# A post-norm layer with attention and 64 experts: wo and z fetched in attention's last pair, shared units moved ahead, the last norm inside the experts' block

## The chip, the cores and the metric

The kernel runs on one core of a Trainium2 chip. The time is the device time of one execution in microseconds (us), as the median over runs on the same inputs; lower is better. Before the change it is 2542.3 us, the median of three runs (2539.97 to 2544.57).

A core has five engines that matter here: PE (TensorE, the matmuls), DVE (VectorE), ACT (ScalarE), POOL (GpSimd) and SP (SyncE, which here only issues DMAs and waits). Each runs its own instructions in order and meets the others at semaphores.

## The reference

One layer on x of 2048 tokens by 512. Attention has 16 heads of 128; the norm stands behind each of the two sums, and has no weights.

```python
scores = jnp.einsum('biph,biqh->biqp', k, q)
masked = scores * mask - jnp.float32(10000000000.0) * (1.0 - mask)
attn = jax.nn.softmax(masked / jnp.sqrt(jnp.float32(d_head)), axis=-1)
z = jnp.einsum('biqp,biph->biqh', attn, v)
out = jnp.einsum('df,bqf->bqd', W_O, z_flat)
...
x = _layernorm(x + attention(x, W_K, W_Q, W_V, W_O))
x = _layernorm(x + ffn(x, gate_w, w1, w2, w3, sw1, sw2, sw3))
```

In `ffn` a softmax over 64 experts picks 6 for each token. An expert takes its first 128 tokens, computes `silu(x w1) * (x w3)` (352 wide) and from it `w2`, and the result is added to the token's row with its gate. A shared expert, 704 wide, is added for every token.

## The kernel before

All large products are made at the precision of fp32 from three matmuls: each operand is split into a rounded part "hi" and the rest "lo", and the passes are hi*hi, lo*hi and hi*lo. The hi part is a copy on ACT; the lo part is a subtraction on DVE, which needs it. So an operand that comes from memory goes DMA, ACT, DVE, PE.

The program has three blocks, one behind the other, with a barrier of all engines between them.

**Attention.** The heads go as 8 pairs, and in each pair the queries as 4 chunks of 512. A table of steps written by hand (`attention_plan`) sets the order on every engine: projections ("job"), scores and their exponentials, "turns" (transposes of the probabilities, which ACT copies as `pT_hi`, L428, and DVE completes as `pT_lo`, L512) and the products with v (L653). The last pair has no projections of a next pair beside it, so its last stretch is turns and products alone. z goes to `z_dram`, tile by tile.

**Projection, routing, experts** (`route_and_experts`). POOL first makes constants (up to L994) for which PE waits. SP fetches the first tile of z (L1081) and `w_o` in 8 groups of two heads; ACT splits z (L1200) and then the groups (L1192), DVE behind it (L1614, L1609). Then PE takes 16 tiles of 128 tokens: the output projection (L1385, 48 matmuls a tile), the norm, the routing and the scattering of rows. Tile 1 of z is fetched once `z_lo` of tile 0 is made. Behind the tiles stand 8 "lead" units of the shared expert, for 4 of the 16 tiles.

Then comes a loop of 4 bodies with 22 units each: 16 experts ("e") and 6 shared units ("s", a half of the shared expert for one tile), in the order `PATTERN = "eeseeseeees" * 2`. A unit on PE is its up products (L1473), the down products of the unit before (L1513), and the transposes of the next unit's rows (L1449) and of its activations (L1454). The experts' weights stream through 8 raw slots: SP fetches a piece (L1133), ACT and DVE split it. Which step fetches and splits which piece stands in a table (`pieces_of_step`); those of the next body's first expert, and at the very start of the loop seven `EARLY` ones, come ahead. POOL adds each expert's result to `sums_dram` by an indirect DMA (L1059) and each shared tile's by a plain one (L1066), one behind the other.

**The last norm** (`combine`). SP loads the 16 tiles of `sums_dram` (L1910). For groups of four tiles DVE measures (L1930, L1934), takes ACT's square root (L1918) through six small steps to 1/sqrt (L1942 to L1958), and normalises (L1963). ACT issues the stores (L1921).

## Time and profile before

| | us |
|---|---|
| median of three runs | 2542.3 |
| profiled execution | 2545.8 |
| its span | 2543.9 |
| PE busy in it | 2438.9 (96%) |
| DVE busy | 1738.1 (68%) |
| ACT busy | 1425.4 (56%) |
| last matmul of the attention block ends | 1620.4 |
| first matmul of the projection | 1635.43 |
| last matmul of all ends | 2498.6 |
| SP starts to load for the last norm | 2509.97 |

The profile is one execution. Its times count from the span's start. In a row of the timeline stand the start, the duration, the engine, the line, what is written and read, and in brackets the idle time before it and what ended it. A busy engine can be waited for or not; a time in which PE is idle is the first thing to look for, because PE is busy for 96% of the span.

### The profile page before, as it was taken

How to read it: one execution, taken by the hardware profiler on the slowest of the kernel's cores; microseconds unless marked ns; L12 is line 12 of the kernel's file. 1: busy time of each engine (PE TensorE's matmuls, PEld its weight loads, DVE VectorE, ACT ScalarE, POOL GpSimd, SP SyncE). 2: the span in 40 equal slices, each digit the busy share in tenths (PEclk: the TensorE clock that was granted, in tenths of full speed). 3: DMA queues.
4: the chain of work that ended last, by engine and by line, in shares of the span. 5: the costliest groups of instructions: out<-in, count | busy, mean ns of one | idle time of the engine just before them, and what ended most of it. 6: DMA issues, size and time to landing. Idle time of an engine off the chain costs nothing. (4 is left out here: it accounts for less than half of the span.)

```text
span 2543.9 us, 40857 instructions
## 1 busy us (share of the span) xinstructions
PE 2438.9 (96%) x14202; PEld 2117.1 (83%) x14202; DVE 1738.1 (68%) x3656; ACT 1425.4 (56%) x3199; POOL 346.6 (14%) x366
## 2 busy tenths in 40 slices
PE   6999999999999999999999999799999999999992
PEld 5888888888888888888888888588889988898982
DVE  4666666566567567657567566578758887888884
ACT  3555455455456456446456455455447776777771
POOL 0000000000000000000000000167621211222121
PEclk9999999999999999999999999899999999999996
DMA  7421411421330331322322220488659999999995
GB/s 263 134 63 57 140 59 56 131 69 28 124 106 26 127 95 37 124 67 65 120 74 65 82 90 26 151 287 315 221 152 310 307 298 291 307 309 305 312 295 153
DMA packets 193421, 397.00 MB, mean 156 GB/s; under 512 B 23674, under 2 KB 73210, under 8 KB 182977
## 3 DMA queue, kind: packets, MB, share of 16 engines
q1 hardware_dynamic: 163456, 330.69, 38.6%
q0 software_dynamic: 27456, 59.51, 10.0%
q10 hardware_dynamic: 2304, 4.20, 0.4%
q8 instruction: 114, 1.87, 0.3%
q14 instruction: 91, 0.74, 0.1%
HBM read 296.45 MB, written 106.48 MB: 158 GB/s over the span
## 5 line engine op out<-in xcount | busy, mean ns | idle before, releaser
L428 ACT ACTIVATE pT_hi<-turned 128x512 fp32r<-128x512 f32 (+3 forms) x640 | 334.2, 535 | 270.9 <-PE turned L638 268.5
L417 ACT ACTIVATE probs<-bank,neg_max 128x512 f32<-128x512 f32 (+3 forms) x640 | 396.6, 626 | 109.5 <-DVE neg_max L506 104.5
L512 DVE TENSOR_TENSOR pT_lo<-turned,pT_hi 128x512 fp32r<-128x512 f32 (+3 forms) x640 | 377.5, 603 | 75.1 <-ACT pT_hi L428 71.7
L498 DVE TENSOR_REDUCE max_part<-bank 128x1 f32<-128x512 f32 (+2 forms) x576 | 345.2, 620 | 96.0 <-PE bank L621 84.0
L608 PE MATMUL bank<-x_sb,w_hi 128*128 128x512 f32 x1024 | 323.4, 397 | 20.1 <-ACT ident_bf L393 13.4
L638 PE MATMUL turned<-ident,probs 128*128 128x128 f32 x2176 | 329.2, 273 | 0.1
L638 PEld LDWEIGHTS turned<-ident,probs 128*128 128x128 f32 x2176 | 264.4, 141 | 49.2 <-PE bank L597 0.3
L653 PE MATMUL z_ps<-pT_hi,v_hi 128*128 128x512 f32 (+3 forms) x640 | 255.0, 398 | 2.5 <-DVE pT_lo L512 1.9
L621 PE MATMUL bank<-k_lo,q_hi 128*128 128x512 f32 (+2 forms) x640 | 254.3, 397 | 0.0
L621 PE MATMUL bank<-k_hi,q_hi 128*128 128x512 f32 (+2 forms) x640 | 253.3, 396 | 0.0
L1764 DVE TENSOR_TENSOR up_lo<-w_raw,up_hi 128x704 fp32r<-128x704 f32 x256 | 217.3, 887 | 39.2 <-ACT up_hi L1256 38.1
L608 PEld LDWEIGHTS bank<-x_sb,w_hi 128*128 128x128 f32 x1024 | 189.8, 190 | 57.5 <-issue 13.4
L653 PE MATMUL z_ps<-pT_hi,v_lo 128*128 128x512 f32 (+3 forms) x640 | 233.8, 365 | 0.0
L621 PE MATMUL bank<-k_hi,q_lo 128*128 128x512 f32 (+2 forms) x640 | 233.7, 365 | 0.0
L653 PE MATMUL z_ps<-pT_lo,v_hi 128*128 128x512 f32 (+3 forms) x640 | 233.2, 364 | 0.0
L283 POOL DMA_DIRECT2D inv_dram<-inv x64 | 35.0, 546 | 1353.1 <-DVE inv L524 1353.1
L608 PE MATMUL bank<-x_sb,w_lo 128*128 128x512 f32 x512 | 200.9, 392 | 0.0
L597 PE MATMUL bank<-w_hi,x_sb 128*128 128x256 f32 x1024 | 193.8, 285 | 1.7 <-ACT probs L417 1.7
L1256 ACT ACTIVATE up_hi<-w_raw 128x704 fp32r<-128x704 f32 x250 | 184.8, 785 | 3.2 <-DMA w_raw<-in_w 3.1
L597 PEld LDWEIGHTS bank<-w_hi,x_sb 128*128 128x128 f32 x1024 | 164.1, 193 | 3.9 <-DVE probs L471 2.1
L1059 POOL DMA_INDIRECT sums_dram<-y_sb,token x64 | 110.7, 1730 | 390.4 <-DMA sums_dram<-y_sb,token 252.7
L597 PE MATMUL bank<-w_lo,x_sb 128*128 128x256 f32 x512 | 145.6, 284 | 0.0
(202 smaller groups left out, 5150.4 us busy)
## 6 DMA issues: line engine op xcount, KB each, us to landing
w_raw<-in_w SPq DMA_DIRECT2D x256, 352.0 KB, 5.7
x_sb<-x_parts SPq DMA_DIRECT2D x62, 1024.0 KB, 6.1
w_raw<-in_w SPq DMA_DIRECT2D x128, 256.0 KB, 5.6
rows_in<-gathered_x SPq DMA_DIRECT2D x64, 263.5 KB, 5.7
spread_sb<-inv_dram POOLq DMA_DIRECT2D x64, 256.0 KB, 3.5
z_dram<-z_sb SPq DMA_DIRECT2D x64, 256.0 KB, 2.3
z_raw<-z_dram SPq DMA_DIRECT2D x16, 1024.0 KB, 5.1
w_raw<-in_w_qkv SPq DMA_DIRECT2D x32, 384.0 KB, 8.6
```

The costliest lines, as they stand in the source:

```text
L417: nc.scalar.activation(probs[:, u % 2, r, kc * CHUNK:kc * CHUNK + used], bank[:, job_at["s", h, c, r, kc] % BANKS, 0:used], ACT.Exp, bias= ...
L428: nc.scalar.activation(pT_sb[0][:, n % TURNS, lo_col:], turned[:, n % TURNS, lo_col:], ACT.Copy).then_inc(turn_hi, 1)
L498: nc.vector.reduce_max(max_part[:, row % ROWS, kc:kc + 1], bank[:, job % BANKS, 0:used], axis=AX_X).then_inc(part_done, 1)
L512: nc.vector.tensor_tensor(pT_sb[1][:, n % TURNS, lo_col:], turned[:, n % TURNS, lo_col:], pT_sb[0][:, n % TURNS, lo_col:].bitcast(F32), AL ...
L597: mark = nc.tensor.matmul(dst[:, t * 2 * DH:(t + 1) * 2 * DH], x_sb[:, a, dt, rows_], w_sb[b][:, dt, 4 * DH:], start=(dt == 0 and (a, b) = ...
L608: mark = nc.tensor.matmul(dst, w_sb[a][:, dt, first:first + DH], x_sb[:, b, dt, :], start=(dt == 0 and (a, b) == PASSES[0]), stop=(dt == D ...
L621: mark = nc.tensor.matmul(dst[:, 0:width], q_sb[a][:, h, r * P:(r + 1) * P], k_sb[b][:, h, kc * CHUNK:kc * CHUNK + width], start=(a, b) == ...
L638: mark = nc.tensor.transpose(turned[:, n % TURNS, r * P:(r + 1) * P], probs[:, u % 2, r, j * P:(j + 1) * P], ident[:])
L653: mark = nc.tensor.matmul(z_ps[:, first * P:], v_sb[a][:, j, h * DH:(h + 1) * DH], pT_sb[b][:, n % TURNS, first * P:], start=(j == 0 and ( ...
L1059: nc.gpsimd.indirect_dma_start(sums_dram, bass.IndirectOffsetOnAxis(ap=token4[:, n:n + 1], axis=0), y_sb[:, n % 2], None, bounds_check=las ...
L1256: nc.scalar.activation(dst_of(0, n % 2, p, up_w, down_w), raw_of(raw, q % SLOTS_RAW, p), ACT.Copy).then_inc(w_hi, 1)
L1764: nc.vector.tensor_tensor(dst_of(1, n % 2, p, up_w, down_w), raw_of(raw, q % SLOTS_RAW, p), dst_of(0, n % 2, p, up_w, down_w).bitcast(F32) ...
```

## The change

It has three parts.

**1. Room and an early start.** The SBUF tensors of the stages are laid out in one function, `rooms`, so that `wo_raw`, `z_raw` and the split z and wo lie over attention's x, w, k and probabilities. In attention's last pair SP fetches all of `w_o` behind the last job, waits for the stores of z and fetches z's first tile. ACT splits that tile in 4 parts and the first two of the 8 groups of wo between its turns; DVE makes their rests between its own. The other six groups are split in the second block. The wait for `gate_w` goes from PE's start to the first logits.

On ACT, at the end of attention; before (`probs` are the exponentials, `pT_hi` the turns):

```order
L428 ACTIVATE pT_hi<-turned 128x384
L417 ACTIVATE probs,sums<-bank,neg_max 128x512 x2
L428 ACTIVATE pT_hi<-turned 128x256
L428 ACTIVATE pT_hi<-turned 128x128
L428 ACTIVATE pT_hi<-turned 128x512 x13
L428 ACTIVATE pT_hi<-turned 128x384
```

And after:

```order
L514 ACTIVATE pT_hi<-turned 128x384
L523 ACTIVATE z_hi<-z_raw 128x512
L503 ACTIVATE probs,sums<-bank,neg_max 128x512 x2
L514 ACTIVATE pT_hi<-turned 128x256
L523 ACTIVATE z_hi<-z_raw 128x512
L514 ACTIVATE pT_hi<-turned 128x128
L523 ACTIVATE z_hi<-z_raw 128x512
L514 ACTIVATE pT_hi<-turned 128x512
L523 ACTIVATE z_hi<-z_raw 128x512
L514 ACTIVATE pT_hi<-turned 128x512 x5
L531 ACTIVATE wo_hi<-wo_raw 128x1024
L514 ACTIVATE pT_hi<-turned 128x512 x2
```

Six splits (the second wo group follows) now stand among the turns; in the second block ACT begins with wo's group 2.

**2. Units.** `PATTERN` is turned by one place, so each body begins with a shared unit; the table of pieces is turned with it, and 2 pieces in place of 7 are early. The tile of each body's first shared unit is fetched by SP two units before the body before ends, behind a wait for the up products of that body's fifth shared unit. POOL's adds of shared tiles come at other places (`tile_after`), so that three experts' adds are last instead of a shared one.

On PE, where the loop begins; before (the first two rows end the last lead unit, `rows_in` are the rows of the first expert's tokens):

```order
L1454 MATMUL t_even<-ident,h_sb 128x128 x2
L1454 MATMUL t_even<-ident,h_sb 96x128
L1449 MATMUL t_odd<-ident,rows_in 128x128 x4
L1473 MATMUL h_even<-up_hi,eT_hi 128x352
L1473 MATMUL h_even<-up_lo,eT_hi 128x352
```

And after, with the end of the unit, 17 rows further on:

```order
L1596 MATMUL t_even<-ident,h_sb 128x128 x2
L1596 MATMUL t_even<-ident,h_sb 96x128
L1615 MATMUL h_even<-s_up_hi,sT 128x352
L1615 MATMUL h_even<-s_up_lo,sT 128x352
...
L1615 MATMUL h_even<-s_up_hi,sT 128x352
L1591 MATMUL t_odd<-ident,rows_in 128x128 x4
L1655 MATMUL ys_ps<-s_down_hi,hT_hi 128x512
```

The transposes of the first expert's rows stood directly ahead of its up products; now a whole up part of a shared unit goes ahead of them.

**3. The last norm** is in the second block, without a barrier ahead of it. SP itself waits for POOL's adds, loads, and issues the stores. The groups are 4, 4, 4, 2 and 2 tiles. ACT normalises tiles 0 to 13 as `inverse * x + shift`, DVE the last two; one of the six steps is folded into another and one makes the shift.

On DVE, for one group; before:

```order
L1942 TENSOR_SCALAR varc<-mvc 128x4
L1945 RECIPROCAL guessc<-rootc 128x4
L1948 TENSOR_TENSOR newton_partc<-guessc 128x4
L1930 BN_STATS statsc<-sums_in 128x6
L1951 SCALAR_TENSOR_TENSOR newton_partc<-newton_partc,varc 128x4
L1955 TENSOR_SCALAR newton_partc<-newton_partc 128x4
L1958 TENSOR_TENSOR inversec<-newton_partc,guessc 128x4
L1934 BN_AGGR mvc<-statsc 128x2
L1963 TENSOR_SCALAR yc<-sums_in,mvc,inversec 128x512
```

And after:

```order
L2011 BN_STATS statsc<-sums_in 128x6
L2026 RECIPROCAL guessc<-rootc 128x4
L2015 BN_AGGR mvc<-statsc 128x2
L2029 TENSOR_TENSOR newton_partc<-guessc 128x4
L2011 BN_STATS statsc<-sums_in 128x6
L2032 SCALAR_TENSOR_TENSOR newton_partc<-newton_partc,varc 128x4
L2015 BN_AGGR mvc<-statsc 128x2
L2036 SCALAR_TENSOR_TENSOR inversec<-newton_partc,guessc 128x4
L2011 BN_STATS statsc<-sums_in 128x6
L2040 SCALAR_TENSOR_TENSOR shiftc<-mvc,inversec 128x4
```

The steps now stand singly between measurements, and no normalising row stands between the groups: it has gone to ACT.

The diff, cut to its core:

```diff
+def rooms(nc, ctx):
+    with ExitStack() as part:
+        x_sb = sb("x_sb", [P, 2, DT, CHUNK], F32R, part)
+        w_raw = sb("w_raw", [P, 3, 6 * DH], F32, part)
+        w_sb = [sb(f"w_{n}", [P, DT, 6 * DH], F32R, part) for n in ("hi", "lo")]
+        k_sb = [sb(f"k_{n}", [P, 2, SEQ], F32R, part) for n in ("hi", "lo")]
+        probs = sb("probs", [P, 2, RPC, SEQ], F32, part)
+    with ExitStack() as part:
+        wo_raw = sb("wo_raw", [P, HEADS, DM], F32, part)
...
@@ attention: tables of the added splits
+        z_hi_part = {(0, 3, 13): 0, (0, 3, 14): 1, (0, 3, 15): 2, (1, 3, 0): 3}
+        z_lo_part = {(1, 3, 1): 0, (1, 3, 2): 1, (1, 3, 3): 2, (1, 3, 4): 3}
+        wo_hi_group = {(1, 3, 5): 0, (1, 3, 7): 1}
+        wo_lo_group = {(1, 3, 6): 0, (1, 3, 9): 1}
@@ attention, SP, behind the last job
+                            for g in range(HEADS // GROUP):
+                                sp.dma_start(room.wo_raw[:, g * GROUP:(g + 1) * GROUP], w_o[:, g * GROUP:(g + 1) * GROUP]
+                                             ).then_inc(begun.wo_in[g], 16)
+                            for n in range(2):
+                                sp.wait_ge(z_out[n], 8 * n_units * PAIRS + 16)
+                            sp.dma_start(room.z_raw[:], z_dram[0]).then_inc(begun.z_in, 16)
@@ route_and_experts
-    PATTERN = "eeseeseeees" * 2
+    PATTERN = "seeseeeseee" * 2
-    LEAD_SPLITS = {4: EARLY[0:2], 5: EARLY[2:4], 6: EARLY[4:5]}
-    LATE_SPLITS = EARLY[5:]
+    LEAD_SPLITS = {4: EARLY}
@@ POOL
-            tile_after = {5 - 1: 0, 10 - 1: 1, NE - 1: 2}
+            tile_after = {1: 0, 7: 1, 12: 2}
@@ SP
-            load_z(0, 0)
-            for g in range(HEADS // GROUP):
-                sp.dma_start(wo_raw[:, g * GROUP:(g + 1) * GROUP], w_o[:, g * GROUP:(g + 1) * GROUP]
-                             ).then_inc(wo_in[g], 16)
             sp.wait_ge(z_lo, 1)
             load_z(0, 1)
...
-            tile_step = {unit_of["s", 0]: (0, -1), unit_of["s", 2] - 2: (1, -1), unit_of["s", 4] - 2: (2, unit_of["s", 1])}
+            sp.wait_ge(up_ready, lead_unit(5) + 1)
+            load_tile(FIRST, tile_slot(0))
+            tile_step = {unit_of["s", 2] - 2: (1, -1), unit_of["s", 4] - 2: (2, unit_of["s", 1]),
+                         NU - 2: (NST, unit_of["s", 5])}
...
+            for n in range(2):
+                sp.wait_ge(y_stored[n], (16 * NE // 2) * BODIES)
+                sp.wait_ge(ys_stored[n], slot_count(BODIES - 1, 2 - n, 16))
+            for t in range(TILES):
+                sp.dma_start(sums[:, t], sums_dram[t * P:(t + 1) * P]).then_inc(loaded[t], 16)
@@ ACT
-            split_z(0, 0)
-            for g in range(HEADS // GROUP):
+            for g in range(FIRST_GROUPS, HEADS // GROUP):
                 split_wo(g)
...
+            for g, tiles_ in enumerate(ENDS):
+                act.wait_ge(mean_ready, tiles_[-1] + 1)
+                part = slice(tiles_[0], tiles_[-1] + 1)
+                nc.scalar.activation(roots[:, part], end_mv[:, part, 1], ACT.Sqrt, bias=end_eps[:]).then_inc(roots_ready, 1)
+                if g:
+                    act.wait_ge(newton_step, END_STEPS * g)
+                    for t in ENDS[g - 1]:
+                        end_normalise(t)
```

## Rows read from the trace of the kernel before

**Rows 1.** The page, part 1: busy time, share of the span, instructions.

```profile
PE 2438.9 (96%) x14202; PEld 2117.1 (83%) x14202; DVE 1738.1 (68%) x3656; ACT 1425.4 (56%) x3199; POOL 346.6 (14%) x366
```

**Rows 2.** Windows: length, busy PE, PEld, DVE, ACT, POOL, granted clock, DMA share, GB/s.

```profile
1600.00:1610.00 10.00, 9.41 (x50) 7.87 (x50) 5.87 (x12) 4.19 (x8) 0.11 (x1) 0.83 0.10 28
1610.00:1620.00 10.00, 10.00 (x62) 8.49 (x62) 5.92 (x10) 4.63 (x9) 0.97 (x2) 1.00 0.11 26
1635.43:1647.94 12.51, 12.51 (x48) 9.95 (x48) 8.86 (x10) 8.56 (x8) 0.00 (x0) 0.88 0.75 298
```

**Rows 3.** Timeline across the blocks' border: start, duration, engine, line, idle before.

```profile
1620.12 0.27 PE L653 MATMUL z_ps<-pT_hi,v_lo 128*128 128x128 f32 x1
1625.05 0.32 SPq L1081 DMA_DIRECT2D z_raw<-z_dram  x1
1626.58 0.14 POOL L994 IOTA mine_i<- 128x16 int32 x1
1629.84 1.91 ACT L1200 ACTIVATE z_hi<-z_raw 128x2048 fp32r<-128x2048 f32 x1 [10.37 <-DMA z_raw<-z_dram]
1631.86 2.29 DVE L1614 TENSOR_TENSOR z_lo<-z_raw,z_hi 128x2048 fp32r<-128x2048 f32 x1 [6.30 <-ACT z_hi L1200]
1632.55 1.06 ACT L1192 ACTIVATE wo_hi<-wo_raw 128x1024 fp32r<-128x1024 f32 x1 [0.80 <-DMA wo_raw<-in_w_o]
1633.83 1.06 ACT L1192 ACTIVATE wo_hi<-wo_raw 128x1024 fp32r<-128x1024 f32 x1 [0.22 <-DMA wo_raw<-in_w_o]
1635.43 0.77 PE L1385 MATMUL o_ps<-wo_hi,z_hi 128*128 128x512 f32 x1 [15.03 <-DVE wo_lo L1609]
```

**Rows 4.** Timeline, PE, from tile 0 to tile 1 of the projection.

```profile
1647.55 0.39 PE L1385 MATMUL o_ps<-wo_hi,z_lo 128*128 128x512 f32 x1
1649.78 0.50 PE L1385 MATMUL o_ps<-wo_hi,z_hi 128*128 128x512 f32 x1 [1.84 <-DVE z_lo L1614]
```

**Rows 5.** Waits over the whole program: who, for what, sum, count, mean.

```profile
PE h_even L1473 <- issue: 6.0, 4, 1.5
ACT up_hi L1256 <- DMA w_raw<-in_w: 3.1, 5, 1.5
```

**Rows 6.** Timeline near the first body's end: fifth shared unit's up, SP's step.

```profile
2009.58 0.40 PE L1473 MATMUL h_odd<-s_up_hi,sT 128*128 128x352 f32 x1
2015.87 0.33 SPq L1144 DMA_DIRECT2D rows_in<-gathered_x  x1
```

**Rows 7.** Timeline, the experts' end.

```profile
2496.84 1.55 POOL L1059 DMA_INDIRECT sums_dram<-y_sb,token  x1 [4.27 <-ACT y_sb L1321]
2498.16 0.40 PE L1513 MATMUL ys_ps<-s_down_hi,hT_lo 96*128 96x512 f32 x1
2502.25 0.92 POOL L1066 DMA_DIRECT2D sums_dram<-ys_sb  x1 [3.85 <-DMA sums_dram<-y_sb,token]
2509.97 8.10 SPq L1910 DMA_DIRECT2D sums_in<-sums_dram  x16
```

**Rows 8.** Timeline, the last norm, and one of the experts' results on ACT.

```profile
2495.39 0.68 ACT L1321 ACTIVATE y_sb<-y_ps,gate 128x512 f32<-128x512 f32 x1
2512.50 0.69 DVE L1930 BATCH_NORM_STATS2 statsc<-sums_in 128x6 f32<-128x512 f32 x1 [2.39 <-DMA sums_in<-sums_dram]
2513.33 0.67 DVE L1930 BATCH_NORM_STATS2 statsc<-sums_in 128x6 f32<-128x512 f32 x1
2516.64 1.28 ACT L1918 ACT_TABLE_LOAD   x1 [20.57 <-DVE mvc L1934]
2517.94 0.30 ACT L1918 ACTIVATE rootc<-mvc,epsc 128x4 f32<-128x4 f32 x1
2537.02 0.16 DVE L1942 TENSOR_SCALAR varc<-mvc 128x4 f32<-128x4 f32 x1
2538.06 0.16 DVE L1948 TENSOR_TENSOR newton_partc<-guessc 128x4 f32<-128x4 f32 x1
2538.86 1.92 DVE L1963 TENSOR_SCALAR yc<-sums_in,mvc,inversec 128x512 f32<-128x512 f32 x4
```

More of the change, by code:

```diff
@@ L1 @@
+from collections import namedtuple
 from contextlib import ExitStack
@@ L76, with first_sems, sem @@
+def first_sems(nc, ctx):
+    def sem(name):
+        return ctx.enter_context(nc.semaphore(name))
+    return FirstSems(sem("z_in"), sem("z_hi"), sem("z_lo"), [sem(f"wo_in{n}") for n in range(HEADS // GROUP)],
+                     sem("wo_hi"), sem("wo_split"))
 ORDER = (
@@ L438, in body @@
                         turn(i, *step[2:])
+                        if last and step[2:] in z_hi_part:
+                            first_z_hi(i, z_hi_part[step[2:]])
+                        if last and step[2:] in wo_hi_group:
+                            first_wo_hi(i, wo_hi_group[step[2:]])
                     if step[0] == "wsplit" and not last:
@@ L542, in body @@
                         low(i, *step[2:])
+                        if last and step[2:] in z_lo_part:
+                            first_z_lo(z_lo_part[step[2:]])
+                        if last and step[2:] in wo_lo_group:
+                            first_wo_lo(wo_lo_group[step[2:]])
                     if step[0] == "inverse":
@@ L742, in route_and_experts @@
     assert EARLY == list(range(EARLY[0], NQ))
-    LEAD_SPLITS = {4: EARLY[0:2], 5: EARLY[2:4], 6: EARLY[4:5]}
-    LATE_SPLITS = EARLY[5:]
-    assert all(pieces[q][0] % 2 for q in LATE_SPLITS) and not any(pieces[q][0] % 2 for q in EARLY[:5])
+    LEAD_SPLITS = {4: EARLY}
+    assert not any(pieces[q][0] % 2 for q in EARLY)
     SLOTS_RAW = 8
@@ L875, in route_and_experts @@
         t_at = {job: n for n, job in enumerate(tjobs)}
+        z_in, z_hi, z_lo, wo_in, wo_hi, wo_split = begun
         waited = sem("waited3")
@@ L936, in route_and_experts @@
         ys_stored = [sem(f"ys_stored{n}") for n in range(2)]
+        eps_ready = sem("eps_ready")
+        loaded = [sem(f"loaded{t}") for t in range(TILES)]
+        stats_ready = sem("stats_ready")
+        mean_ready = sem("mean_ready")
+        roots_ready = sem("roots_ready")
+        newton_step = sem("newton_step")
+        y_ready = sem("y_ready")
+        y_ready_dve = sem("y_ready_dve")
+        stored = sem("stored")
         block = ctx.enter_context(nc.Block())
@@ L1327, in body @@
                         turned(i, ("x", 0))
-                    if first and u == 0:
-                        for q in LATE_SPLITS:
-                            split_first(q)
                     if not (first and u < 2):
@@ L1336, in body @@
                     silu(i, u)
+                    if first and u == 0:
+                        for m in range(2):
+                            act.wait_ge(rows_left[m], rows_of(TILES - 2 + m))
+                        for m in range(NB):
+                            act.wait_ge(x1_stored[m], 16 * TILES // NB)
+                        for m in range(2):
+                            act.wait_ge(t_stored[m], 32 * TILES // 2)
                     if u + 1 < NU and UNITS[u + 1][0] == "e":
@@ L1943, in invert @@
                 if n == 1:
-                    dve.wait_ge(rooted, g + 1)
-                    ins = nc.vector.reciprocal(guess[:, part], root[:, part])
+                    dve.wait_ge(roots_ready, g + 1)
+                    ins = nc.vector.reciprocal(guess[:, part], roots[:, part])
                 if n == 2:
@@ L1978, in _ @@
-                    if g < GROUPS:
-                        mean(t)
-                    if g:
-                        normalise(t - GROUP)
+                    end_measure(t)
+                    steps = (FOUR if len(tiles_) == 4 else TWO)[n] if g else ()
+                    for m in steps[:1]:
+                        invert(g - 1, m)
+                    end_mean(t)
+                    for m in steps[1:]:
+                        invert(g - 1, m)
+            for n in range(END_STEPS):
+                invert(len(ENDS) - 1, n)
```

339 lines of the change are left out of this document (167 added, 172 removed).

## The prediction

> **What bounds the kernel now.** I read page part 1 first: PE is busy for 96% of the span, ACT and DVE for much less [rows 1]. So the change can only gain where PE stands idle and after its last matmul. Those places come from PE's idle times in the timeline: 15.03 us between attention and projection, 1.84 us ahead of tile 1 [rows 3, 4], 6.0 us in four waits at the body starts [rows 5], and the end, from the last matmul at 2498.56 to 2543.9 [rows 7, 8]. That is 68 us of idle time. The three parts of the change are aimed at these places and leave PE's matmuls as they are, in number and shape.
>
> A difference within 0.2%, about 5 us, cannot be told from no change. The sum is made against the profiled execution, 2545.8 us. The median of the runs is 2542.3, so 3.5 is taken off at the end.
>
> **A. Attention's tail.** ACT gets 4 splits of 128x512 and 2 of 128x1024, DVE as many. From the rows, a 128x1024 split on ACT is 1.06 and z's 128x2048 is 1.91, on DVE 2.29 [rows 3]; a quarter of these is about 0.5 and 0.6. ACT gets some 4 x 0.5 + 2 x 1.06 = 4.1 us, DVE 4 x 0.6 + 2 x 1.2 = 4.8. In 1600 to 1620 ACT is busy for 4.2 and 4.6 of each 10 us, DVE for 5.9 and 5.9 [rows 2], so there is room. But turns come in a chain PE, ACT, DVE, PE, and a split in front of one makes it late. In 1600 to 1610 PE is already idle for 0.6 us; later it is never idle [rows 2], and has turns made ahead. Laying the tail end to end with these durations I get +1.5. The bounds are 0 and +4 (all of ACT's part shows, as the chain is through ACT).
>
> **B. The gap between the blocks.** The last matmul of attention ends at 1620.12 + 0.27 = 1620.4. The first of the projection is at 1635.43, after DMA of z (issued 1625.05), z_hi at 1629.84, z_lo at 1631.86, and the wo splits behind them [rows 3]. After the change z's tile 0 and four heads of wo are split by then. What is left stands in front of all of them: z's last store and the barrier, which let SP begin at 1625.05, and POOL's constants, made from there to 1626.58 + 0.14 = 1626.72 [rows 3], for which PE still waits. So the first o_ps is at about 1626.8, 8.6 earlier. Does wo keep up? ACT makes a group in 1.27 (1632.55 to 1633.83 [rows 3]). Six groups from 1625.1 are done at 1632.7, DVE's last one about 1.2 later, 1633.9. PE comes to the eighth group after 14 of 16 heads of a tile that takes 12.51 [rows 2], at 1626.8 + 10.9 = 1637.7. No wait. The bounds are -9 (POOL's constants a little earlier) and -7 (a late group or barrier costs 1.5). The granted clock of tile 0 was 0.88 [rows 2], below 1 because PE starts at 1.2 GHz after the idle time; I leave that as it is, since 6.4 us of idle time remain.
>
> **C. The wait ahead of tile 1.** 1.84 us for z_lo [rows 4], which comes because tile 1 is fetched only after tile 0's z_lo, and z_lo is behind ACT's eight groups. Now the fetch goes out at 1625.5. Landed 4.8 later (1625.05 to 1629.84 [rows 3]) it waits for ACT's six groups, 1632.7; z_hi 1.91 and z_lo 2.29, started 2.02 behind z_hi [rows 3], make 1637.0. Tile 0 ends at 1626.8 + 12.5 = 1639.3. The wait goes: -1.8, with -1 as the other bound.
>
> **D. Body starts.** PE waited four times 1.5 us "on issue" for the first h_even [rows 5]: the transposes of the expert's rows were directly in front of its up products, so that ACT and DVE had to copy them with PE standing. Now a shared unit's up part stands between, 3.8 us long (24 matmuls at 0.16, as h_even and h_odd go in the loop). All of it goes: -6.0, with -5 as the bound. What takes its place? The first tile of the next body is fetched at SP's step NU-2, behind a wait for the fifth shared unit's up. On the rows of before that up began at 2009.58 and lasts 3.8 us, done by 2013.5, and SP comes to the step at 2015.87 [rows 6]. SP is therefore not held, by 2.3 us, and the row loads and weights queued behind are not late. Seven early pieces become two, so five are fetched and split a unit later. The pieces then have a whole shared unit to land in.
>
> **E. The experts' end.** The last matmul ends at T = 2498.56. POOL issues the last expert's add at 2496.84, T - 1.7, and the shared add goes out when that has landed, 2502.25, T + 3.7: one indirect add takes 5.4. Then come the shared add, the barrier and the block's start, and SP loads at 2509.97, T + 11.4 [rows 7]. After, the last three units are experts. The second to last add lands at T + 3.7 as before; the last takes another 5.4, T + 9.1; SP itself waits for it and loads at T + 9.2. So -2.2: an indirect add takes the place of the plain one, and eats most of what the barrier gives. The bounds are -3.2 (add of 4.4) and -0.6 (add of 7).
>
> **F. The last norm.** Before, from L = 2509.97 to 2543.9 is 33.9, and the last normalising ends at 2538.86 + 1.92 = 2540.78, 3.1 before the end [rows 8]. DVE is the engine in the chain. After, per tile it measures in 0.83 (2512.50 to 2513.33) and per group makes six steps of 0.20 (four from 2538.06 to 2538.86) [rows 8]. Group 0 is measured by L + 6.7, where ACT's root was asked for at 2516.64 [rows 8]. Then groups of 4, 4, 2 and 2 cost 4 x 0.83 + 1.2 = 4.5, 4.5, 2 x 0.83 + 1.2 = 2.9 and 2.9: L + 11.1, 15.6, 18.5, 21.4. The last group's steps with its root take 1.84 (2537.02 to 2538.86), DVE's two last tiles 2 x 0.48, and 3.1 is added as before [rows 8]: L + 27.3. So -6.7. ACT's part is 14 tiles at about 0.57 (y_sb, the same shape, is busy for 0.68 [rows 8], and back to back a little less), 2.3 a group against DVE's 4.5. The loads take 8.1 to issue [rows 7], and the last measurement is at L + 20, so they aren't late. Bounds -8 (store's tail shorter) and -5 (DVE and ACT each slower by a quarter in places).
>
> **Sum.** +1.5 - 8.6 - 1.8 - 6.0 - 2.2 - 6.7 = -23.8. Of the profiled 2545.8 this leaves 2522.0; of the median 2518.5. All bounds together are 0 - 9 - 1.8 - 6 - 3.2 - 8 = -28 and 4 - 7 - 1 - 5 - 0.6 - 5 = -14.6, so 2514 to 2528.
>
> **Rivals.**
> R1, the end gives less. The last indirect add is as slow as 7 us (E -0.6), and F gives -3 only, because the small steps, strung singly between measurements, each wait for the one before. For it: each step takes what the one before has written, and one that starts too early stands. Against it: a measurement of 0.69 or its second part stands between them, longer than the 0.20 from one step to the next [rows 8]. 1.5 - 8.6 - 1.8 - 6.0 - 0.6 - 3 = -18.5, or 2524.
>
> R2, the weights come late. Five pieces less are ahead at the loop's start. For it: ACT did wait for w_raw in the loop, so the stream has no large reserve. Against it: only five times, for 3.1 us in all [rows 5]. If each of the five missing pieces costs one such wait of 1.5, and the five existing ones double, 7.5 + 3.1 = 10.6 come on top: 2529.
>
> R3, ACT holds the last norm. The first root waits for a table load of 1.28, the root following 1.30 behind its start [rows 8]. If the load held ACT for twice as long, DVE, which asks for the first reciprocal at about L + 8.5, would stand for 1.4 us; and if the normalising went at y_sb's full 0.68 a tile [rows 8] and not at 0.57, four tiles would end 0.4 later. That is -22.0, or 2520.3. The Trainium skill, "ScalarE: Activation LUTs", section "What ACT_TABLE_LOAD costs", speaks for it: it counts a drain of 1.38 us with each load, 2.66 in all, and some 93 ns for each operand that is one value per partition, of which the new normalise has two. By that rule the sum is -22.0. The trace of before shows the load and no drain behind it, 1.30 to the root, so my sum goes without.
>
> R4, the side above. The splits in attention's tail stand in the chain one behind another, 4.1 + 4.8 = 8.9 us, and their holes drop PE to 1.2 GHz for the 23 us that the tail has left, which doubles them: 8.9 + 23 = +32 in place of +1.5. 2518.5 + 30.4 = 2549, slower. It decides from +25.3, where A eats all other terms. For it: 1600 to 1610 is granted 0.83 with 0.6 us idle [rows 2]. Against it: in the next 10 us the clock is 1.00 and PE is never idle, with ACT busy for less than half.
>
> R5, the room isn't free when it should be: the fetches into attention's old room wait until the last jobs are done, and would hold up SP. The last pair's stores come before the z fetch on SP's queue, and nothing that PE needs stands behind them. Should z's parts be late by more than the turns allow, B falls to -5, and the sum to -20.2: 2522.
>
> **How the numbers follow.** The forecast's own case (2514 to 2523) has 0.62, R1 0.14, R3 0.08, R5 0.05, R2 0.07 and R4 0.04. 2518.5 is the time of the likeliest. The range of 2511 to 2528 takes in R1, R3 and R5 and the bounds, and a little below, since an estimate of six terms can be short on both sides; R2 and R4 are left out with 0.11 and the rest of the tails. Faster by over 0.2% (below 2537.2) is all but R4 and half of a further mishap: 0.94. Within 0.2%: 0.03, slower: 0.03.
>
> **What would show it.** First o_ps 6.4 us behind the last z_ps, not 15; no wait for z_lo at tile 1; no "issue" wait at h_even; attention's last z_ps at 1621 to 1622 and not past 1625, at a granted clock near 1; the first sums_in issue at T + 9.2 with the last indirect add landing just before; 27.3 us from there to the end, with DVE free of idle times over 0.7. It would be wrong if the tail's holes grow, if ACT's w_raw waits in the loop go past 10 us, or if y_ready of tile 13 comes behind DVE's last two tiles.

## The result, and the profile after

| | before | changed |
|---|---|---|
| median of the runs, first comparison (5 and 5 runs) | 2542.3 us | 2525.9 us (2518.3 to 2530.3) |
| ratio, 95% interval | | 0.993 (0.9906 to 0.9954) |
| median, second comparison (17 and 6 runs) | 2546.2 | 2523.0 (2520.5 to 2527.6) |
| ratio, 95% interval | | 0.9913 (0.9888 to 0.9938) |
| span of the profiled execution | 2543.9 | 2528.5 |

The change is faster by 16 us in one comparison and 23 in the other, where 23.8 were forecast. The two ratios agree within their intervals. The runs of the changed kernel lie 7 to 12 us apart in a comparison; what this spread goes with is shown below.

Two corrections to what stands ahead. The last number of the waits in [rows 5] is the longest one and not the mean. And `PATTERN` is not only turned by one place. The strings in the diff show it: before, a period has experts in runs of 2, 2 and 4 between shared units, after it 2, 3 and 3. And the third shared tile's add now stands ahead of the body's last three experts.

**The span by terms.** T is the end of the last matmul, L is SP's first load for the last norm.

| stretch | before | after | difference | forecast |
|---|---|---|---|---|
| start to the last z_ps (A) | 1620.39 | 1620.35 | 0.0 | +1.5 |
| to the first o_ps (B) | 15.04 | 6.39 | -8.7 | -8.6 |
| to T (C and D) | 863.1 | 864.5 | +1.3 | -7.8 |
| T to L (E) | 11.4 | 11.8 | +0.4 | -2.2 |
| L to the end (F) | 33.9 | 25.5 | -8.5 | -6.7 |

So the start and the norm gave what they should, or more, and the middle gave nothing. PE is now busy for 97%, with the same number of matmuls as in [rows 1]:

```profile
PE 2440.2 (97%) x14202; PEld 2119.3 (84%) x14202; DVE 1731.5 (68%) x3651; ACT 1436.3 (57%) x3217; POOL 350.9 (14%) x366
```

The border of the blocks, timeline of the changed kernel (answers [rows 3]):

```profile
1620.08 0.27 PE L778 MATMUL z_ps<-pT_hi,v_lo 128*128 128x128 f32 x1
1626.54 0.14 POOL L1114 IOTA mine_i<- 128x16 int32 x1
1626.74 0.80 PE L1525 MATMUL o_ps<-wo_hi,z_hi 128*128 128x512 f32 x1 [6.38 <-POOL mine_i L1114]
```

The tail that ends there, as a window (its columns as in [rows 2]), is at full clock:

```profile
1610.00:1620.00 10.00, 9.97 (x62) 8.20 (x60) 7.47 (x12) 5.48 (x10) 0.55 (x2) 1.00 0.10 26
```

PE waits for POOL's last constant and nothing else, and tile 1 starts without a wait: in the changed kernel's timeline no idle time over 0.25 us stands between this row and the lead units. That is [rows 4] gone.

The waits of the whole program (answer to [rows 5]): for whom, sum, count, longest.

```profile
POOL sums_dram L1179 <- DMA sums_dram<-y_sb,token: 284.5, 45, 8.4
PE t_even L1596 <- DVE h_sb L1929: 10.0, 3, 5.0
ACT up_hi L1388 <- DMA w_raw<-in_w: 3.8, 6, 1.3
```

The row "h_even <- issue" of [rows 5] is gone: the body starts no longer wait, as forecast. The weights, which rival R2 suspected, are as they were (3.1 before, 3.8 now). But PE's wait for h_sb has grown from 4.0 us in two waits to 10.0 in three, and the first row, POOL waiting for its own DMA 45 times, is the largest wait of any engine in the loop. Both rows stood in the trace of before as well; I had not read them:

```profile
POOL sums_dram L1059 <- DMA sums_dram<-y_sb,token: 252.7, 42, 8.3
PE t_even L1454 <- DVE h_sb L1792: 4.0, 2, 3.0
```

From the first o_ps to T, PE's idle time went from 20.3 us to 19.2 only, and its busy time from 842.8 to 845.3. That is the +1.3 of the table, where 7.8 us of idle time were to go.

**What the 10.0 us are.** The longest but one of them, at 2049, in the timeline of the changed kernel, POOL, ACT and PE:

```profile
2030.17 0.91 POOL L1186 DMA_DIRECT2D sums_dram<-ys_sb  x1 [6.66 <-DMA sums_dram<-y_sb,token]
2032.57 0.68 ACT L1445 ACTIVATE y_sb<-y_ps,gate 128x512 f32<-128x512 f32 x1
2038.41 2.00 POOL L1179 DMA_INDIRECT sums_dram<-y_sb,token  x1 [7.32 <-issue]
2044.89 0.69 ACT L1445 ACTIVATE y_sb<-y_ps,gate 128x512 f32<-128x512 f32 x1 [5.51 <-issue]
2049.16 0.87 PE L1596 MATMUL t_even<-ident,h_sb 128*128 128x128 f32 x3 [4.00 <-DVE h_sb L1929]
```

Read it from the top. POOL's adds go to the same tensor, so in the kernel each waits until the one before has landed: a shared tile's at 2030.17 lands after 7.4 us, and an expert's follows at 2038.41, 8.2 us behind it. There are two result buffers (`y_sb`). ACT comes to the next result at 2039.4 (2044.89 less the idle 5.51), but its buffer is held by the add issued at 2038.41, and that lands 6.4 us later, at 2044.8. ACT stands until then; behind it in its queue is the act_sb of the next unit, behind this DVE's h_sb, and PE waits 4.0 us for that. Then PE starts at 1.2 GHz, seen in the granted clock of 0.50:

```profile
2048.00:2053.00 5.00, 3.84 (x14) 3.79 (x15) 4.97 (x13) 3.58 (x8) 1.56 (x1) 0.50 0.99 273
```

So such a wait costs more than its idle time: the matmuls behind it come every 0.29 us in place of 0.16 for 4 us, which by these numbers is some 1.9 us more (an estimate).

**The end**, timeline of the changed kernel (answers [rows 7]):

```profile
2486.92 1.61 POOL L1179 DMA_INDIRECT sums_dram<-y_sb,token  x1 [4.33 <-issue]
2490.81 0.39 PE L1655 MATMUL y_ps<-down_hi,hT_lo 96*128 96x512 f32 x1
2492.58 1.55 POOL L1179 DMA_INDIRECT sums_dram<-y_sb,token  x1 [4.05 <-ACT y_sb L1445]
2498.24 1.56 POOL L1179 DMA_INDIRECT sums_dram<-y_sb,token  x1 [4.10 <-DMA sums_dram<-y_sb,token]
2503.03 8.25 SPq L1312 DMA_DIRECT2D sums_in<-sums_dram  x16
```

The adds of the last three experts are issued 5.66 us apart. Each lands 4.7 to 4.9 us after its issue, and the next goes out 0.8 us behind that. The last but one starts at T + 1.4 and not at T - 1.7, because the third last is under way until 2491.8. The bracket of its row names ACT's y_sb, but the result that ended at 2492.5 on ACT is the last expert's; this add's own was ready at 2488.7:

```profile
2488.04 0.68 ACT L1445 ACTIVATE y_sb<-y_ps,gate 128x512 f32<-128x512 f32 x1
2491.85 0.69 ACT L1445 ACTIVATE y_sb<-y_ps,gate 128x512 f32<-128x512 f32 x1 [3.13 <-PE y_ps L1655]
```

SP loads at once when the last has landed, without a barrier. What the barrier gave was eaten by one link of this chain.

**The last norm**, DVE and ACT at its end (answers [rows 8]):

(the row of four and the row of 0.80 are the same group, the latter its last)

```profile
2509.71 1.28 ACT L1507 ACT_TABLE_LOAD   x1 [17.17 <-DVE mvc L2015]
2511.01 0.30 ACT L1507 ACTIVATE rootc<-mvc,epsc 128x4 f32<-128x4 f32 x1
2520.19 2.92 ACT L1499 ACTIVATE yc<-sums_in,shiftc,inversec 128x512 f32<-128x512 f32 x4
2522.31 0.80 ACT L1499 ACTIVATE yc<-sums_in,shiftc,inversec 128x512 f32<-128x512 f32 x1
2523.01 0.28 ACT L1507 ACTIVATE rootc<-mvc,epsc 128x2 f32<-128x2 f32 x1
2523.33 0.17 DVE L2026 RECIPROCAL guessc<-rootc 128x2 f32<-128x2 f32 x1 [1.52 <-ACT rootc L1507]
2524.31 1.00 DVE L2062 TENSOR_SCALAR yc<-sums_in,mvc,inversec 128x512 f32<-128x512 f32 x2
```

DVE is through all measurements, and the steps of the group before the last, at L + 18.8 where I had L + 21.4: 2.6 us sooner, since the small steps between measurements cost about 0.1 and not 0.2 us each. At the very end ACT is late, as R3 had it: the root stands behind four normalisings, and DVE waits 1.52, which makes the last group's steps 0.7 longer than forecast.

### The profile page after: what moved, and what is told of

It is laid out like the page before. It is cut to its first block and busy times, and to the rows that moved or that the text cites. A ratio compares the mean times of both kernels' runs of the same rounds, so it can differ in the third digit from the quotient of the medians.

```text
span 2528.5 us, 40864 instructions
## 1 busy us (share of the span) xinstructions
PE 2440.2 (97%) x14202; PEld 2119.3 (84%) x14202; DVE 1731.5 (68%) x3651; ACT 1436.3 (57%) x3217; POOL 350.9 (14%) x366
## 5 line engine op out<-in xcount | busy, mean ns | idle before, releaser
L1179 POOL DMA_INDIRECT sums_dram<-y_sb,token x64 | 116.2, 1816 | 398.8 <-DMA sums_dram<-y_sb,token 284.5
```

Source lines behind the costliest of these rows:

```text
L1179: nc.gpsimd.indirect_dma_start(sums_dram, bass.IndirectOffsetOnAxis(ap=token4[:, n:n + 1], axis=0), y_sb[:, n % 2], None, bounds_check=las ...
```

## The experiments

Theory A, formed from the rows above: **POOL's adds to the sums are a chain that bounds the loop beside PE.** A body has 16 experts' adds and 3 shared ones. From the first to the last of the loop's 76 adds the changed kernel takes 591.4 us, 7.89 a link, so 19 links are 149.8 us. PE's body without the waits is 146.6 (experiment 9; 148.4 in experiment 1, with the 1.5 of the old body start). Taking PE's wait away leaves it waiting for the chain. The mean of a link alone doesn't prove this, as it is the loop's time divided by the adds, whichever of the two bounds it. The brackets say more: in the changed kernel 57 of the 76 issues follow a landing, in that of before 53, and some that name ACT or "issue" do so too, like those at 2038.41 and 2492.58 above. The experiments that shorten the chain decide. Theory B: the new order is a gain, and the microseconds were lost to the weights or the DMA engines. In the third theory a single place of the order is at fault (experiment 2).

The main numbers of the profiled executions, all described below. A link is the mean distance between POOL's 76 issues in the loop; where PE waits for nothing it is the loop's pace and not what the chain needs. The last column is the median of the runs; that of before lay between 2542 and 2548 in the several comparisons.

| kernel | T | link | L | span | median |
|---|---|---|---|---|---|
| before | 2498.6 | 7.83 | 2509.97 | 2543.9 | 2546 |
| changed | 2491.2 | 7.89 | 2503.03 | 2528.5 | 2525.9 |
| changed, again | 2479.5 | 7.72 | 2493.38 | 2518.7 | 2523.0 |
| order back | 2481.2 | 7.75 | 2488.96 | 2515.0 | 2521.8 |
| third tile's add later | 2494.8 | 7.92 | 2504.98 | 2530.5 | 2536.1 |
| shared adds out | 2474.7 | 7.64 (9.09 between its 64 adds) | 2483.69 | 2509.3 | 2512.3 |
| four buffers | 2476.8 | 7.64 | 2486.85 | 2512.6 | 2524.8 |
| order alone | 2497.5 | 7.85 | 2515.82 | 2549.8 | 2550.5 |
| plain writes | 2477.2 | 7.59 | 2481.88 | 2507.4 | 2509.1 |

From L to the end the kernels of this table with the new norm take 25.3 to 26.0 us, so L decides, and L is when the chain ends.

**1. The order of before, back in the changed kernel.**

```diff
-    PATTERN = "seeseeeseee" * 2
+    PATTERN = "eeseeseeees" * 2
...
-            tile_after = {1: 0, 7: 1, 12: 2}
+            tile_after = {5 - 1: 0, 10 - 1: 1, NE - 1: 2}
```

(with the tables of pieces and tiles that belong to it)

> The changed kernel with its second part undone: the order of units, the table of pieces, the early pieces and the places of the shared adds are those of before; the early start and the last norm inside the block stay. Theory A (POOL's chain of adds to the sums, one at a time, bounds the loop beside PE, and the new order made it late): the loop is as before, with 6 us of waits at body starts and about 4 us for h_sb; the start keeps its -10.5 us; at the end the last indirect add lands at T + 3.7 and SP loads at about T + 7.5, so 3.9 better than before; the norm is 8.4 better. Sum -22.8: 2519.5 us, faster than the whole change. Theory B (the new order is a gain, and its missing microseconds were lost elsewhere): about 6 us slower than the whole change, 2532.

Measured: 2521.8 (ratio to before 0.9916, 0.9891 to 0.9941), against 2525.9 and 2523.0 of the whole change: no slower in either of its comparisons. Its profile has the four body starts' 1.5 us back and no wait for h_sb at all. Theory B's 2532 is out. The end of its chain:

```profile
2479.48 1.55 POOL L1180 DMA_INDIRECT sums_dram<-y_sb,token  x1 [4.29 <-ACT y_sb L1451]
2484.86 0.92 POOL L1187 DMA_DIRECT2D sums_dram<-ys_sb  x1 [3.82 <-DMA sums_dram<-y_sb,token]
2488.96 8.54 SPq L1310 DMA_DIRECT2D sums_in<-sums_dram  x16
```

L is at T + 7.8 here, 4.0 sooner after T than in the changed kernel. With a shared unit last, the last expert's add is on its way before T. From the first o_ps to T this profile takes 853.1 us, where that of before, with the same loop, took 863.1, of which 1.8 are the wait ahead of tile 1 and 4.0 waits for h_sb. So much do single executions differ.

**2. The third shared tile's add later.**

```diff
-            tile_after = {1: 0, 7: 1, 12: 2}
+            def tile_after(i):
+                return {1: 0, 7: 1, 12 if i == BODIES - 1 else 15: 2}
```

> The changed kernel with the third shared tile's add behind the body's last expert in place of behind the thirteenth, in the first three bodies (as before the change); nothing else. If the place is the fault (the add stands ahead of a run of three experts, which have two result buffers): the waits of PE for h_sb at the three body ends (4.0, 5.0, 1.1 us in the profile) go, about 2517. If the whole chain is at its limit (19 adds of 7.8 us are 148 us, as long as PE's body): waits of the same size come up a few units later, 2521 to 2526.

Measured: 2536.1 (ratio 0.9969, 0.9954 to 0.9983), slower than either case had it. The waits came up elsewhere, at 2095.8, 2248.3 and 2401.6, and are of 5.6, 4.1 and 4.2 us. So the place wasn't the fault. Why the median is 10 us above the changed kernel's and not equal isn't settled: the profiled execution is only 2 us longer, and shows only that the links were long (7.92).

**3. The shared adds taken out of the chain.** The loop's shared tiles are written to a tensor of their own and left out of the result.

```diff
-                s = tile_after.get((n - 1) % NE)
+                s = tile_after.get((n - 2) % NE)
...
-                pool.wait_ge(y_stored[n % 2], i * (16 * NE // 2) + 16 * (n // 2 + 1))
                 wait_apart(pool, waited4, ys_read, tile_count(i, s))
-                pool.dma_start(sums_dram[bass.ds((i * NST + (FIRST + s)) * P, P)], ys_sb[:, tile_slot(s)],
-                               accum_op=ALU.add).then_inc(ys_stored[tile_slot(s)], 16)
+                pool.dma_start(apart_dram[bass.ds((i * NST + s) * P, P)], ys_sb[:, tile_slot(s)]
+                               ).then_inc(ys_stored[tile_slot(s)], 16)
```

> The changed kernel without 12 links of the chain: the loop's shared tiles are written to a tensor of their own, without accumulating and without waiting for or holding up the experts' adds (their part is left out of the result). Theory A (the chain): no wait for h_sb over 1 us, the matmuls end 6 to 9 us earlier, the last add starts when the one before has landed, at about T + 3, so SP loads at T + 8 and not T + 11.8: some 2513. Rival (the waits come from the weights' stream, or the DMA engines being full): as the bytes are nearly the same, no more than 3 us change, 2523 or over.

Measured: 2512.3 (ratio 0.9875, 0.9853 to 0.9896), where theory A said 2513 and its rival 2523 or over. The waits for h_sb went to 0.2 us in one. POOL now waits for ACT's results instead:

```profile
POOL sums_dram L1179 <- DMA sums_dram<-y_sb,token: 224.9, 38, 8.2
POOL sums_dram L1179 <- ACT y_sb L1444: 166.1, 22, 11.1
```

In the changed kernel the second row had 38.2 us in 7 waits. The chain has slack as soon as it is 12 links shorter, with nearly the same bytes moved. The DMA engines are as full as before: their share from 1900 to 2470 is 0.99 here and in the changed kernel, at 306 and 302 GB/s. So it isn't full DMA engines by themselves that PE waits for.

**4. The splits of wo and z all in the second block.**

```diff
-FIRST_GROUPS = 2
+FIRST_GROUPS = 0
...
-        z_hi_part = {(0, 3, 13): 0, (0, 3, 14): 1, (0, 3, 15): 2, (1, 3, 0): 3}
+        z_hi_part = {}
...
+            split_z(0, 0)
             for g in range(FIRST_GROUPS, HEADS // GROUP):
                 split_wo(g)
```

> The changed kernel, with wo and z's first tile fetched in attention's last pair as there, but all of their splits made in the second block. My account: the first o_ps needs z_hi (to 1627.2), z_lo (to 1629.5) and the first group's rest (to 1630.7), so it starts 4.0 us later than in the changed kernel; tile 1 does not wait; attention's end moves by less than 0.5 us, since the splits there cost nothing: 2530. Rival (the splits in the tail cost the 1.5 us forecast, hidden in the noise): only 2.5 us slower, with attention's last product 1.5 us earlier.

Measured: 2530.0 (ratio 0.9936, 0.9918 to 0.9954), whose interval overlaps those of the whole change, so the gap must decide. It is 10.5 us in place of 6.4, as my account has it:

```profile
1625.64 1.91 ACT L1332 ACTIVATE z_hi<-z_raw 128x2048 fp32r<-128x2048 f32 x1 [5.86 <-PEq L222]
1627.66 2.29 DVE L1755 TENSOR_TENSOR z_lo<-z_raw,z_hi 128x2048 fp32r<-128x2048 f32 x1 [1.80 <-ACT z_hi L1332]
1631.23 0.77 PE L1526 MATMUL o_ps<-wo_hi,z_hi 128*128 128x512 f32 x1 [10.53 <-DVE wo_lo L1750]
```

But the tail isn't free either, which is the rival's point. Over all profiles, attention's last z_ps ends at 1621.8 on average in the ten executions with splits in the tail (1620.4 to 1622.4), and at 1620.5 in the four without (1619.5 to 1621.6): 1.3 us, near the +1.5 of the forecast, though single executions of one group differ by 2. The holes show where: with the splits PE waits 1.26, 1.21 and 0.50 us for pT_lo, without them 1.26 and 0.69. So the net gain of splitting early is about 3 us, and that of fetching early 4.5.

**5. The changed kernel again.**

> The changed kernel itself, unedited, beside the three others on the same chip, since runs of it and of before spread over 10 us: 2526 to 2529, with 1 to 4 waits for h_sb of 1 to 6 us in the profile, and SP's first load for the last norm at T + 11 to 12 (T is the end of the last matmul).

Measured: 2523.0, some 3 us quicker than expected. This profile has waits for h_sb of 1.1 and 0.7 us only and a T 11.7 us earlier than the first one, but L is at T + 13.9. PE ran ahead and the chain ended when it did: from the first o_ps to L it is 864.9 us, against 860.8 with the order of before (experiment 1). The links took 7.72 here and 7.89 in the first profile; 75 x 0.164 = 12.3 us. The chain began 2.4 later here, which leaves 9.9, and the two spans differ by 9.8. Such differences are the spread of the runs.

**6. Four result buffers.**

```diff
-                nc.scalar.activation(y_sb[:, n % 2], y_ps[:], ACT.Copy, scale=gate[:, n:n + 1]).then_inc(y_read, 1)
+                nc.scalar.activation(y_of[n % 4], y_ps[:], ACT.Copy, scale=gate[:, n:n + 1]).then_inc(y_read, 1)
```

> The changed kernel with four buffers for the experts' results in place of two, so that PE can be four experts ahead of POOL's adds; the adds still go one at a time. Theory A (the chain of adds is the bound: 76 of them at 7.89 us from 1906.8 to 2498.2): PE's waits for h_sb go and the last matmul comes 6 to 9 us earlier, but the chain goes on at its own pace, so SP's first load comes no more than 3 us earlier, at T + 16 or more: 2523 to 2526. Rival (two buffers are the fault, and the chain has room): T 6 to 9 us earlier and the load with it, 2517 to 2519.

Measured: 2524.8 (2514.3 to 2530.9; ratio 0.9920, 0.9893 to 0.9947), the changed kernel's own time. PE has no wait for h_sb left. The profiled execution was a quick one, at 2514.3 the lowest of its six runs, with L at T + 10.1 and not T + 16; it can't tell theory A from its rival. The median speaks for A. But the runs spread over 16.6 us and the lower end of the interval is some 2519 us, which the rival had, so this experiment alone doesn't settle it.

**7. The new order alone, in the kernel before.**

> The kernel before with the second part of the change alone (order of units, table of pieces, early pieces, places of the shared adds). My forecast of that part was -6.0 us. Theory A: PE's four waits at the body starts go, but PE's body then is 146.9 us while 19 adds take 7.75 to 7.9 each, 147 to 150; waits for h_sb of 6 us or more come in their place, and the end is later by some 4 us, as three experts' adds in a row follow the last products: 0 to +5 on before. Rival (the order only hurts together with the other parts): 4 to 6 us faster than before.

Measured: 2550.5 (ratio 1.0021, 1.0002 to 1.0041), by the medians 4.3 us slower than before. My forecast of this part had been 6.0 faster.

```profile
2059.74 0.87 PE L1453 MATMUL t_even<-ident,h_sb 128*128 128x128 f32 x3 [4.10 <-DVE h_sb L1788]
2357.29 0.87 PE L1453 MATMUL t_even<-ident,h_sb 128*128 128x128 f32 x3 [2.69 <-DVE h_sb L1788]
2497.10 0.40 PE L1512 MATMUL y_ps<-down_hi,hT_lo 96*128 96x512 f32 x1
2515.82 8.08 SPq L1904 DMA_DIRECT2D sums_in<-sums_dram  x16
```

The body starts' 6.0 us are gone and the waits for h_sb are 6.8, where before had 4.0. From the first o_ps to T it takes 860.5 us, 2.6 less than before; but with the barrier still there L is at T + 18.3, 6.9 more than in [rows 7].

**8. The new norm alone, in the kernel before.**

> The kernel before with the third part of the change alone: the last norm inside the experts' block, with its groups of 4, 4, 4, 2, 2 and ACT normalising; the start and the order of units are those of before. By the other runs the norm itself takes 25.5 to 26.0 from SP's first load to the end in place of 33.9 (-8.1), and with the order of before the load is at T + 7.8 in place of T + 11.4 (-3.6): -11.7, so about 2534 to 2535 beside a before of 2546. If parts gain more together than alone, less than 8 us.

Measured: 2534.4 (ratio 0.9952, 0.9933 to 0.9972), as expected. L is at T + 7.9.

**9. Plain writes in place of adds.** Nothing is accumulated in the loop, so the result lacks the sums; the order and the waits of the writes are kept.

```diff
-                    bounds_check=last_row, compute_op=ALU.add).then_inc(y_stored[n % 2], 16)
+                    bounds_check=last_row).then_inc(y_stored[n % 2], 16)
...
-                               accum_op=ALU.add).then_inc(ys_stored[tile_slot(s)], 16)
+                               ).then_inc(ys_stored[tile_slot(s)], 16)
```

> The changed kernel with every add of the loop (experts' rows and shared tiles) made a plain write: same bytes written, same order, each still waiting for the one before, but nothing read and added in memory (so the sums are left out of the result). Theory A: a link gets shorter (7.0 us to landing becomes 4 to 5.5), PE's waits for h_sb go, SP's first load is at T + 8 to 10: about 2512 to 2515, as with the shared adds apart. If the length of a link comes from the issue and the full DMA engines and not from the accumulating, nothing changes: 2522 to 2528.

Measured: 2509.1 (ratio 0.9851, 0.9832 to 0.9870), a little better than expected, with L at T + 4.7 and not T + 8 to 10. Its five runs lie within 0.6 us (2508.7 to 2509.3), where the changed kernel's spread over 7 to 12. PE has no wait for h_sb, and 34 of the 76 issues follow a landing. The DMA issues of the two, median us to landing; first the changed kernel, then this one:

```profile
sums_dram<-y_sb,token POOLq DMA_INDIRECT x64, 7.4
```

```profile
sums_dram<-y_sb,token POOLq DMA_INDIRECT x64, 5.8
```

The accumulating makes a link about 1.6 us longer. And the spread goes with the chain as the bound: it is 0.6 us here and 2.8 in experiment 3, where the chain had slack though its expert links still accumulate.

**10. Four buffers, the order of before, and the constants.** PE's wait for POOL's constants goes behind the first tile's projection:

```diff
                     project(i, k, range(0, COUNTED))
+                if k == 1:
+                    pe.wait_ge(pool_const, 5)
...
-            pe.wait_ge(pool_const, 5)
             for k in range(TILES):
```

> The changed kernel with the order of before (as in the first of these experiments), four buffers for the experts' results, and PE's wait for POOL's constants moved behind the first tile's projection (and nine heads of the second's). The constants held the first o_ps from about 1625.1 to 1626.7, so 1.6 us less there; the four buffers take what waits for h_sb are left in some runs (0 in the profile, by the spread of runs up to 6 us); the chain bounds still. About 2519, and the spread of the runs under 8 us. If the chain ends as late as it did, no better than 2521.

Measured: 2518.6 (2517.5 to 2525.1; ratio 0.9898, 0.9872 to 0.9923). The gap before the first o_ps:

```profile
1627.32 0.77 PE L1527 MATMUL o_ps<-wo_hi,z_hi 128*128 128x512 f32 x1 [5.29 <-PEq L222]
```

5.3 us, so 1.1 saved and not 1.6: PE's own start in the block comes next. This version beats the kernel before. Against the changed one it is 4.5 us lower by the two medians of the same comparison, but the intervals of the two ratios overlap, so a gain over it isn't shown.

**11. The shared tiles apart, added back at the end.** As in experiment 3, and the 12 tiles are brought into the last norm's buffer when PE is done; POOL adds the sums onto them:

```diff
+            for t in range(FIRST, TILES):
+                pool.dma_start(sums[:, t], sums_dram[t * P:(t + 1) * P], accum_op=ALU.add).then_inc(loaded[t], 16)
```

> The changed kernel with the loop's shared tiles written to a tensor of their own (no link in the chain), made whole again at the end: when PE is done SP loads these 12 tiles into the last norm's buffer, while the last adds still land, and for these tiles POOL then issues accumulating DMAs from the sums onto it in place of SP's plain loads (0.9 us each to issue, against 1.1 that DVE takes for a tile). PE's wait for POOL's constants is behind the first tile's projection. Theory A: the chain is 64 links, shorter than PE's time, so the loop is as in the run with the shared adds left out (2512.3), the constants give 1.1 us, and the end is covered: 2511 to 2513. If POOL's issues or landings don't keep up with DVE, or the 12 loads hold up the last adds, the end is 3 to 8 us longer: 2515 to 2520.

Measured: 2523.1 (ratio 0.9908, 0.9891 to 0.9925), slower than either case had it. The loop gave what it should (T at 2475.8), and the end took it back:

```profile
2475.91 6.36 SPq L1318 DMA_DIRECT2D sums_in<-apart_dram  x12
2479.71 1.56 POOL L1180 DMA_INDIRECT sums_dram<-y_sb,token  x1 [4.04 <-DMA sums_dram<-y_sb,token]
2487.90 1.74 SPq L1322 DMA_DIRECT2D sums_in<-sums_dram  x4
2490.07 10.71 POOL L1202 DMA_DIRECT2D sums_in<-sums_dram  x12 [8.80 <-DMA sums_in<-apart_dram]
```

The 12 loads and the last add ran at the same time, and that add took 8.2 us to L where it took 5.1 in experiment 3; with an issue 1.1 later, L is 4.2 later than there. POOL's twelve issues then came late and fed DVE a tile every 1.3 us: 32.5 from L to the end in place of 25.5.

**12. Only each body's third shared tile apart.** The four tiles are brought back as in experiment 11.

```diff
+                if s == 2:
+                    wait_apart(pool, waited4, ys_read, tile_count(i, s))
+                    pool.dma_start(apart_dram[bass.ds(i * P, P)], ys_sb[:, tile_slot(s)]).then_inc(ys_stored[tile_slot(s)], 16)
+                    return
```

> The changed kernel with only each body's third shared tile (four in all) written to a tensor of its own and out of the chain, and added back at the end: SP loads these four tiles into the last norm's buffer when PE is done, and POOL then issues four accumulating DMAs onto them. PE's wait for POOL's constants is behind the first tile's projection. By theory A 18 links of 7.75 us a body are 140 us, below PE's 146.9, so PE should not wait for h_sb, its last matmul ends near 2476, and the last add lands about 9 us later; four POOL issues in place of twelve (which cost 7 us at the end in the run before) stay under DVE's pace: 25.5 to 27 us from SP's load to the end. 2511 to 2515, with a spread of the runs of 3 us or less. If two tiles a body still fill the chain: 2517 or more.

Measured: 2518.0 (2513.9 to 2519.3; ratio 0.9888, 0.9869 to 0.9908). PE has no wait for h_sb, T is at 2475.2: 18 links are short enough. But from L, 2485.47, it is 29.7 us to the end and not 25.5 to 27, because DVE waits for loads (1.75 us in the longest of five such waits). So the time is in the range that was set for a full chain, 2517 or more, but the lost microseconds are at the end and not in the loop. The four runs spread over 5.4 us, where 3 or less were expected. It is level with experiment 10, and as far as the intervals tell, neither is the better.

## Why the prediction was right, and where it wasn't

The time is in the range and the sign is right; the point, 2518.5, is 7.4 below the first median and 4.5 below the second.

- **B and C were right to 0.1 us.** What was left in front of PE (the barrier, then POOL's constants to 1626.7) could be read in [rows 3].
- **A was right on average** (1.3 for 1.5), though the first profile alone shows none of it. One profile can't show 1 us at a place where executions differ by 2. The quarters of z's split were a little longer than I had them, 0.62 to 0.68 us for 0.5 and 0.6.
- **D is the step that failed.** "All of it goes: -6.0" is true of the body starts, but the time came back as waits for h_sb, a slower clock behind them, and a later end of the chain. I looked for what comes late next in SP's queue and the weights, and not in POOL's. The part alone is a loss of 4.3 us by the medians (experiment 7). The row for it was in the trace of before: POOL waited 252.7 us in the loop for its own adds. Read beside it, 19 links by 7.8 us against a body of 148.4 us, minus the 1.5 that I was taking away, would have been the warning.
- **E failed by the same chain** and by one unit, +0.4 us where -2.2 were forecast: I carried "add at T - 1.7" from a body that ends in a shared unit to one that ends in three experts. R1 had the price of a slow last add (7 us), not that the add before it would be late.
- **F was mis-sized, -6.7 for -8.5.** A small step between measurements costs 0.1 us. Of R3's two halves the longer table load didn't show: it took 1.28 us and the root started 1.30 after its start, as before the change. The other did: four normalisings take 2.92, 0.70 apart and 0.80 each where I had 0.57, and DVE stood 1.52 for the root behind them. On that half an estimate from the figures of the Trainium skill, "ScalarE: Activation LUTs", section "What ACT_TABLE_LOAD costs", is 186 + 2 x 93 + 0.833 x 512 = 799 ns for one normalising. The trace agrees with 0.80 us. On the drain of 1.38 us, which that section adds to each load, the measurement decides, and shows none here.
- **R2 is out** (the waits for w_raw are 3.8 for 3.1 us). **R4 is out**: the granted clock in 1610 to 1620 stayed at 1.00. **R5 is out**: SP issued the fetch of z at 1544.5, 50 us before its first split.

**Partly luck.** The two comparisons of the same kernel differ by 7 us, so that one of them comes near 23.8 proves little, and the terms don't bear it out. By the ratios, on 2546 us, the norm alone gives 12 us (experiment 8), with the early start it is 21 (experiment 1), and with the new order 18 or 22. Each of these is uncertain by 5 or 6 us. So the start gave about its forecast 8.9, the norm and its earlier loads more than the 8.9 of E and F together, and the order nothing that can be seen, where D had 6.0. The norm covers a part of what the order didn't give.

What stays open: why the mean link varies from one execution to the next by some 0.2 us, which makes the spread; why experiment 2 lost 10 us and not nothing; and how long 19 links would take if nothing but the chain held them, since no run times the chain alone.

## What to carry to other kernels

An engine that mostly issues DMAs and waits for them is hardly busy (POOL 14% here), so the busy shares don't show it as a bound: add up its links and compare with the loop's period before pricing the removal of a wait on the main engine. The sum alone isn't enough, since it comes out near the period for any engine that keeps up; count also how many of the issues wait for a landing. If a wait of 1.5 us is taken out of a period of 148.4 and a chain takes 145 to 150, as in these profiles, little or nothing is gained, and longer waits with a slow clock behind them may take its place. When the end of a loop is moved, follow the last two or three links of such a chain by name, since what follows the loop begins when the chain ends and not when the matmuls do.

## What the runs showed of the hardware

- An indirect add of 128 rows of 2 KB takes 6.9 to 7.5 us (median) from issue to landing in the loop, where the DMA share is 0.99, and 5.8 there as a plain write (share 0.92). At the end, with a DMA share of 0.31 to 0.34, it lands after 4.7 to 4.9, and the next is issued 5.4 to 5.7 behind it. Beside twelve loads one took 8.1 to land (experiment 11).
- Runs of one kernel spread over 7 to 23 us where all 76 accumulating adds stand in the chain, over 5.4 with 72, over 2.1 and 2.8 with 64, and over 0.6 with plain writes.
- After an idle time of 4.0 us PE is granted 0.50 for some 4 us (changed kernel, at 2049).
